# Own places for the expert results of a routed layer, and a gap behind every indirect transfer of five bodies

## The chip, the cores and the metric

The kernel runs on one core of one Trainium2 chip. The metric is the device time of one execution in microseconds (us), as the median of several runs. The kernel before takes 930.24 us (three runs, 926.34 to 932.70).

## The reference

Two layers on `x` of 4 x 1024 tokens of 128 numbers. Layer 0 is a differential attention times a gate from an FP4-rounded feed-forward; layer 1 is a linear attention times a gate from a mixture of experts. The change lies in the mixture of experts:

```
probs = softmax(x @ wg.T); topk_w, topk_idx = top_k(probs, 2)      # 8 experts, 2 for each token
topk_w = topk_w / sum(topk_w)
h1, h3 = x @ w1[e].T, x @ w3[e].T                                  # 128 -> 256, for each expert e
y[e] = (silu(h1) * h3) @ w2[e].T                                   # 256 -> 128
out = sum over the 2 chosen experts of weight * y[e]
x = x + attention * silu(out)
```

## The kernel before

The program is a row of phases with a barrier between them: setup, project, attention, linear, expert. The linear phase computes the layer-1 attention and the routing. The expert phase does the expert matrices and the final sum.

**Routing by scatter.** The four batches form two sets of two. For each set the tokens, each twice (once for each of its two experts), are sorted by expert into 39 tiles of 128 slots (`SLOTS`), padded for each expert. So there are 78 tiles. A row of 129 numbers (128 of the token and one that names where its result belongs) is written by `scatter_rows` (L932) to its slot in the DRAM tensor `slots`; one indirect transfer on the queue of GpSimd (POOL) writes 128 rows. Each set needs 32 of them. Those of set 0 and the first six of set 1 are issued in the linear phase; the other 26 (the list `later`) are issued in the expert phase.

**Bodies.** A body is six tiles (`BODY`), in two halves of three (`TRIO`); there are 13 bodies, numbered 0 to 12. For each tile s of body b: TensorE transposes the tile (`turn_x`, L1813), multiplies by both up matrices (`up`, L1822), ScalarE takes the tanh (L1769), VectorE makes the hidden tile in two steps (L1678, L1681), TensorE transposes it (`turn_a`, L1833) and multiplies by the down matrix (`down`, L1844), and VectorE copies the result out of PSUM (`keep_y`, L1694). Within a body the steps of neighbouring tiles are interleaved by hand: at step s, TensorE does `up(s)`, `turn_x(s+2)`, `turn_a(s-1)`, `down(s-2)`, in this order.

**Loads.** SyncE (SP) loads the halves of the next body with `load_next(b)`, which calls `load_tiles` (L925): half i of body b+1, once `turn_x` has read the old half and VectorE has copied its destinations (`keep_goal`, L1686). Tiles 36 to 38, the first half of body 6, are the last of set 0; the second half of body 6 is the first that holds rows of set 1. So its load, in `load_next(5, wait_rows=True)`, waits at L1580 for all 26 scatters of the list `later`.

**Sends.** `send(b, i)` on POOL sends the three result tiles of half i of body b to the DRAM tensor `expert_outputs`, with one indirect transfer each (L1636). The results lie in two buffers of three tiles, `y_out[i]`. Before a half is overwritten (in `keep_y`), and before its destinations are copied to `goal_now[i]` (L1631), there is a wait for the transfers of the same half one body earlier (`y_sent[i]`). Slots that hold no token are sent to one of 768 spare rows. The order of the queue of POOL is written out by hand: in bodies 0 to 4 (`EARLY`) some two or three scatters stand ahead of each half's sends, 26 in all, the last three of them ahead of `send(4, 1)`. Bodies 5 to 7 and 8 to 11 are hardware loops, body 12 is written out.

**Hands.** The results of set 0 are read back in four hands of four token tiles while bodies 8 to 11 run (`READY` = 8): SP loads them (`load_y`, L1585), POOL weighs one choice (`weigh_first`, L1642) and adds `x` (`add_x`, L1646), VectorE does the rest (L1698 to L1712), SP stores (`store`, L1589). Four more hands (`last_hands`) come after the last send, and end the kernel. `finish` (L1712) waits for the store of the hand before it.

**Memory.** `xn_all`, `v_all` and `w13_in` are three tiles of 4096 columns, which nothing reads any more in the expert phase.

## Time and profile before

| | us |
|---|---|
| median of 3 runs | 930.24 |
| the profiled execution | 931.66 |
| its span, first to last instruction | 928.8 |
| granted TensorE clock, mean | 0.873 of full |

The expert phase covers the span from 706 us on. The page of the profile gives the busy time of each engine, how each slice of the span looks, and the chain of work that ended last. The timeline lists instructions by start time; the number in brackets is the idle time of that engine just before, with what released it. "remote" there is a releaser that the trace doesn't know.

### The profile page before, as it was taken

Reading aid. Unit: us, or ns where it says so; the run is one execution under the profiler, and the core shown is the slowest. Engines: PE = TensorE matmul, PEld = TensorE weight load, DVE = VectorE, ACT = ScalarE, POOL = GpSimd, SP = SyncE. Lnnn points to the kernel's source line nnn. Section 1 sums busy time; section 2 is a strip of 40 time slices with the busy share of each in tenths; the row PEclk is TensorE's granted clock in tenths of the full one; section 3 lists DMA queues with packets and bytes.
Section 4 is the critical chain, followed back from the end, with each engine's and each line's share of the span. In section 5 each row is a group of like instructions: output and inputs, shape, how many; then the busy total and the mean of one; then the engine's idle time right before and its main releaser. Section 6 shows DMA issues by size and latency. Waiting matters only on the chain. (4 is left out here: it accounts for less than half of the span.)

```text
span 928.8 us, 14563 instructions
## 1 busy us (share of the span) xinstructions
PE 709.9 (76%) x4458; PEld 358.3 (39%) x4459; DVE 613.6 (66%) x1470; ACT 504.4 (54%) x911; POOL 443.6 (48%) x524
## 2 busy tenths in 40 slices
PE   3455539999999999999999956787367777898840
PEld 1234422333333333333333345675244444565520
DVE  3999972786868687868686655787163443467735
ACT  2367656777777777777787823233033332344431
POOL 0244433455656564646565521117713667456653
PEclk9777755999999999999999977778577999899975
DMA  5100029800000000000000010001201222233342
GB/s 131 42 24 23 12 69 191 123 24 23 24 23 23 23 23 23 23 23 16 6 23 24 1 47 24 23 24 41 74 24 40 72 71 63 61 92 114 99 113 59
DMA packets 58770, 45.32 MB, mean 49 GB/s; under 512 B 5960, under 2 KB 53392, under 8 KB 58736
## 3 DMA queue, kind: packets, MB, share of 16 engines
q1 hardware_dynamic: 51392, 34.97, 15.1%
q0 software_dynamic: 4544, 9.35, 3.0%
q10 hardware_dynamic: 2800, 0.58, 0.3%
q8 instruction: 17, 0.28, 0.1%
q14 instruction: 17, 0.14, 0.0%
HBM read 15.72 MB, written 16.59 MB: 35 GB/s over the span
## 5 line engine op out<-in xcount | busy, mean ns | idle before, releaser
L748 ACT ACTIVATE attend_prob<-attend_ps_s 128x1024 f32<-128x1024 f32 (+3 forms) x384 | 293.5, 816 | 95.6 <-PE attend_ps_s L848 93.1
L696 POOL TENSOR_TENSOR attend_prob<-attend_prob,attend_causal 128x256 f32<-128x256 f32 x256 | 202.3, 810 | 178.6 <-ACT attend_prob L748 177.3
L866 PE MATMUL attend_ps_o<-attend_prob,attend_v_slot 128*32 128x512 f32 (+3 forms) x1536 | 167.3, 509 | 0.0
L848 PE MATMUL attend_ps_s<-attend_qk_slot 32*128 32x512 f16 (+3 forms) x768 | 124.6, 339 | 21.9 <-ACT attend_prob L748 16.4
L1636 POOL DMA_INDIRECT expert_outputs<-expert_y_out,expert_goal_now x78 | 75.5, 968 | 64.8 <-issue 27.5
L848 PEld LDWEIGHTS attend_ps_s<-attend_qk_slot 32*128 32x128 f16 x768 | 34.8, 91 | 179.1 <-issue 86.4
L1822 PE MATMUL expert_ps_h<-w,expert_x_t 128*128 x156 | 91.3, 669 | 0.6 <-ACT expert_x_t L1756 0.6
L932 POOL DMA_INDIRECT slots<-rows,slot_index x64 | 61.6, 963 | 56.9 <-issue 56.9
L1769 ACT ACTIVATE expert_tanh<-expert_ps_h 128x256 f32<-128x256 f32 x78 | 30.0, 384 | 97.0 <-PE expert_ps_h L1822 67.1
L1844 PE MATMUL expert_ps_y<-w,expert_hidden_t 128*128 x312 | 54.3, 299 | 19.8 <-DVE expert_y_out L1694 14.1
L1678 DVE SCALAR_TENSOR_TENSOR expert_silu<-expert_tanh,expert_ps_h 128x256 f32<-128x256 f32 x78 | 32.7, 419 | 49.8 <-ACT expert_tanh L1769 30.7
L809 DVE SCALAR_TENSOR_TENSOR attend_hidden<-attend_gate_tanh,attend_ps_gate 128x352 f32<-128x352 f32 x32 | 16.7, 521 | 57.7 <-ACT attend_gate_tanh L752 57.7
L1844 PEld LDWEIGHTS expert_ps_y<-w,expert_hidden_t 128*128 128x128 f32 x312 | 43.0, 199 | 27.9 <-issue 26.1
L411 POOL TENSOR_TENSOR project_parts_k<-project_rotated_k,project_parts_k 128x1024 f16<-128x1024 f32 x8 | 17.1, 2132 | 57.2 <-ACT project_parts_k L453 57.2
L866 PEld LDWEIGHTS attend_ps_o<-attend_prob,attend_v_slot 128*32 128x32 f32 x1536 | 30.6, 108 | 34.6 <-issue 26.9
L1694 DVE COPY expert_y_out<-expert_ps_y 128x128 f32<-128x128 f32 x78 | 22.3, 286 | 25.6 <-remote 16.9
L1307 ACT ACTIVATE linear_qk_square<-linear_ps_c 128x512 f32<-128x512 f32 x16 | 9.5, 592 | 52.7 <-PE linear_ps_c L1411 27.8
L1760 ACT ACTIVATE expert_hidden_t<-expert_ps_a 128x256 f32<-128x256 f32 x78 | 30.2, 388 | 13.8 <-remote 7.4
L1833 PE MATMUL expert_ps_a<-ident,expert_hidden 128*128 128x128 f32 x156 | 31.5, 284 | 7.4 <-DVE expert_hidden L1681 5.0
L496 PE MATMUL project_ps_qkv<-att_w,project_xn_t 128*128 128x384 f32 x64 | 33.6, 689 | 4.4 <-issue 3.7
L1240 POOL TENSOR_TENSOR x<-x,linear_gated 128x1024 f32<-128x1024 f32 x4 | 9.4, 2359 | 53.6 <-DVE linear_gated L1072 53.5
L1681 DVE TENSOR_TENSOR expert_hidden<-expert_silu,expert_ps_h 128x256 f32<-128x256 f32 x78 | 32.8, 420 | 2.7
(252 smaller groups left out, 1367.6 us busy)
## 6 DMA issues: line engine op xcount, KB each, us to landing
attend_qk_slot<-qk_parts SPq DMA_DIRECT2D x16, 512.0 KB
slots<-attend_zeros SPq DMA_DIRECT2D x26, 193.5 KB
x_pairs<-slots SPq DMA_DIRECT2D x26, 193.5 KB
expert_y_in<-expert_outputs SPq DMA_DIRECT2D x8, 512.0 KB, 6.8
xn_all<-project_xn SPq DMA_DIRECT2D x8, 256.0 KB, 2.3
w_in<-L_ffn_w SPq DMA_DIRECT2D x4, 512.0 KB
rows<-rows SPq DMA_DIRECT2D x4, 512.0 KB
out<-expert_result SPq DMA_DIRECT2D x8, 256.0 KB, 2.3
```

Source lines behind the costliest of these rows:

```text
L496: ins = nc.tensor.matmul(qkv4[:, j, 0:3 * C], xn_t[odd][:, j * P:(j + 1) * P], m.att_w[:, 0:3 * C], start=True, stop=True)
L696: nc.gpsimd.tensor_tensor(part, part, bcast(causal, 1, 2), ALU.mult).then_inc(masked[n], 1)
L748: nc.scalar.activation(prob2[k % PROBS][:, :, 0:cols], s2[k % 2][:, :, 0:cols], ACT.Exp, scale=HD ** -0.5).then_inc(exp_made[k], 1)
L848: ins = nc.tensor.matmul(ps_s[k % 2][:, s * QC:(s + 1) * QC - off], qk_slot[slot][rows, T + j * P:T + (j + 1) * P], qk_slot[slot][rows, qc ...
L866: ins = nc.tensor.matmul(ps_o[RB * s:RB * (s + 1), off:QC], v4[slot][:, j, s], prob2[(2 * n + s // 2) % PROBS][:, s % 2, 0:QC - off], star ...
L932: pool.indirect_dma_start(m.slots, bass.IndirectOffsetOnAxis(m.slot_index[g][c][:, j:j + 1], 0), m.rows[c][:, t * ROW:(t + 1) * ROW], None ...
L1636: pool.indirect_dma_start(m.outputs, bass.IndirectOffsetOnAxis(goal_now[i][:, j:j + 1], 0), y_out[i][:, j * P:(j + 1) * P], None).then_inc ...
L1678: nc.vector.scalar_tensor_tensor(out=silu[c], in0=th[c], scalar=1.0, in1=ps_h[c][:, 0:EI], op0=ALU.add, op1=ALU.mult).then_inc(silu_made[s ...
L1681: nc.vector.tensor_tensor(act_e[c], silu[c], ps_h[c][:, EI:2 * EI], ALU.mult).then_inc(a_made[s], 1)
L1822: nc.tensor.matmul(ps_h[s % 3], x_t[s % 3], m.w13[:, ds(expert * (2 * EI), 2 * EI)], start=True, stop=True).then_inc(h_made[s], 1)
L1833: ins = nc.tensor.transpose(ps_a[s % 2][:, c * P:(c + 1) * P], act_e[s % 3][:, c * P:(c + 1) * P], m.ident)
L1844: ins = nc.tensor.matmul(ps_y[:, 0:P], act_t[s % 2][:, c * P:(c + 1) * P], m.w2[:, ds(expert * EI + c * P, P)], start=c == 0, stop=c == 1)
```

## The change

`y_out` becomes one tile `m.y_out` of 78 places of 128 columns, laid over the dead `xn_all`, `v_all` and `w13_in` (now parts of one tile). `keep_y` writes tile 6b+s to its own place, at an address from the loop's counter. The copies to `goal_now` and the waits for `y_sent` in `send` and `keep_y` go; the transfer reads its destinations from `goal`. Every slot has a spare row of its own (9984 rows in place of 768). The order of POOL is written out for all 13 bodies. In bodies 0 to 4 every send and every scatter is followed by `leave_gap`: a clear of the scratch tile `idle` (128 x 256, f32) and a wait for it. `READY` goes from 8 to 9, so the four hands run in bodies 9 to 12, and the last body does a hand too. SP waits for one semaphore for each set in place of one for each half.

```diff
-SPARE = BODY * P
+SPARE = SETS * SLOTS * P
-        READY = -(-SLOTS // SB) + 1
+        READY = -(-SLOTS // SB) + 2
-        y_out = [sb(f"y_out{i}", TRIO * P) for i in range(2)]
-        goal, spare = sb("goal", SETS * SLOTS, U32), sb("spare_row", BODY, U32)
-        goal_now = [sb(f"goal_now{i}", TRIO, U32) for i in range(2)]
+        idle = sb("idle", 2 * P)
+        goal, spare = sb("goal", SETS * SLOTS, U32), sb("spare_row", SETS * SLOTS, U32)
...
-            with eng.Fori(READY, READY + HANDS) as b:
+            with eng.Fori(READY, BODIES - 1) as b:
                 pairs(b, tok=b - READY)
-            for b in range(READY + HANDS, BODIES):
-                pairs(b, last=b == BODIES - 1)
+            pairs(BODIES - 1, last=True, tok=HANDS - 1)
...
-            for i in range(2):
-                sp.wait_ge(y_sent[i], 16 * TRIO * FIRST_SENT[i])
+            sp.wait_ge(y_sent[0], 16 * SLOTS)
...
-            for b in range(READY + HANDS - 1, BODIES - 1):
-                load_next(b)
-                store(0, b - READY - 1)
             for n in range(BODIES - 2 - READY, HANDS):
                 store(0, n)
-            for i in range(2):
-                sp.wait_ge(y_sent[i], 16 * TRIO * BODIES)
+            sp.wait_ge(y_sent[1], 16 * SLOTS)
...
+            def leave_gap():
+                nc.gpsimd.memset(idle, 0.0).then_inc(idled, 1)
+                pool.wait_ge(idled, next(gaps))
+
             def send(b, i):
                 pool.wait_ge(goal_kept[i], b + 1)
-                once(pool, y_sent[i], 16 * TRIO * b)
-                pool.sem_inc(send_go, 1)
-                nc.gpsimd.tensor_copy(goal_now[i], goal[:, ds(BODY * b + TRIO * i, TRIO)]).then_inc(goal_set[i], 1)
-                pool.wait_ge(goal_set[i], b + 1)
                 for j in range(TRIO):
+                    t = BODY * b + TRIO * i + j
                     pool.wait_ge(y_kept[TRIO * i + j], b + 1)
                     pool.sem_inc(send_go, 1)
-                    pool.indirect_dma_start(m.outputs, bass.IndirectOffsetOnAxis(goal_now[i][:, j:j + 1], 0),
-                                            y_out[i][:, j * P:(j + 1) * P], None).then_inc(y_sent[i], 16)
+                    pool.indirect_dma_start(m.outputs, bass.IndirectOffsetOnAxis(goal[:, t:t + 1], 0),
+                                            m.y_out[:, t * P:(t + 1) * P], None).then_inc(y_sent[t // SLOTS], 16)
+                    if b < EARLY:
+                        leave_gap()
...
             for b in range(EARLY):
                 for i in range(2):
                     n = 2 * b + i
-                    scatter_rows(pool, m, later[n * len(later) // (2 * EARLY):(n + 1) * len(later) // (2 * EARLY)], rows_scattered)
+                    for row in later[n * len(later) // (2 * EARLY):(n + 1) * len(later) // (2 * EARLY)]:
+                        scatter_rows(pool, m, [row], rows_scattered)
+                        leave_gap()
                     send(b, i)
-            with pool.Fori(EARLY, READY) as b:
+            for b in range(EARLY, BODIES):
+                hand = 0 <= b - READY < HANDS
+                if hand:
+                    weigh_first(0, b - READY)
                 for i in range(2):
                     send(b, i)
...
+                if hand:
+                    add_x(0, b - READY)
...
             def keep_y(b, s):
                 dve.wait_ge(y_made[s], b + 1)
-                if s % TRIO == 0:
-                    once(dve, y_sent[s // TRIO], 16 * TRIO * b)
-                nc.vector.tensor_copy(y_out[s // TRIO][:, s % TRIO * P:(s % TRIO + 1) * P], ps_y[:, 0:P]).then_inc(y_kept[s], 1)
+                nc.vector.tensor_copy(m.y_out[:, ds((BODY * b + s) * P, P)], ps_y[:, 0:P]).then_inc(y_kept[s], 1)
...
-        m.x, m.xn, m.v = (sb(n, BATCH * T) for n in ("x", "xn_all", "v_all"))
+        m.x, shared = sb("x", BATCH * T), sb("xn_v_w13", 3 * BATCH * T)
+        m.xn, m.v, m.w13_in = (shared[:, i * BATCH * T:(i + 1) * BATCH * T] for i in range(3))
+        m.y_out = shared[:, 0:SETS * SLOTS * P]
```

## Rows read from the trace of the kernel before

**Rows 1.** The page: busy time of each engine (share) xinstructions
```profile
PE 709.9 (76%) x4458; PEld 358.3 (39%) x4459; DVE 613.6 (66%) x1470; ACT 504.4 (54%) x911; POOL 443.6 (48%) x524
```

**Rows 2.** Stretches of the expert phase: from:to, length, busy time by engine, clock, DMA
```profile
714.79:799.08 84.29, 63.20 (x268) 38.19 (x268) 34.05 (x100) 26.44 (x90) 53.88 (x65) 0.92 0.23 66
799.08:834.80 35.72, 35.29 (x174) 22.08 (x173) 22.20 (x65) 16.22 (x57) 19.57 (x25) 1.00 0.28 81
834.80:888.51 53.71, 47.40 (x217) 28.70 (x217) 39.71 (x96) 23.30 (x76) 34.51 (x39) 0.97 0.35 99
```

**Rows 3.** Timeline of POOL, 722 to 726 us: start, us, engine, line, operation, [idle before]
```profile
722.32 0.96 POOL L932 DMA_INDIRECT slots<-rows,slot_index  x1 [0.30 <-issue]
723.29 0.20 POOL L1631 COPY expert_goal_now<-expert_goal 128x3 uint32<-128x3 uint32 x1
724.33 0.97 POOL L1636 DMA_INDIRECT expert_outputs<-expert_y_out,expert_goal_now  x1 [0.84 <-POOL expert_goal_now L1631]
```

**Rows 4.** Waits from 714.79 to 799.08 us: total us, times, longest
```profile
DVE expert_y_out L1694 <- remote: 16.9, 8, 3.7
...
PE expert_ps_y L1844 <- DVE expert_y_out L1694: 14.1, 7, 3.8
```

**Rows 5.** Timelines of TensorE and of VectorE, 728 to 733 us
```profile
728.49 1.12 PE L1822 MATMUL expert_ps_h<-w,expert_x_t 128*128 x2
...
729.53 0.42 DVE L1681 TENSOR_TENSOR expert_hidden<-expert_silu,expert_ps_h 128x256 f32<-128x256 f32 x1
732.31 0.29 DVE L1694 COPY expert_y_out<-expert_ps_y 128x128 f32<-128x128 f32 x1 [2.36 <-remote]
```

**Rows 6.** Timeline of ScalarE and of POOL in the linear phase, 641 to 674 us
```profile
673.41 0.60 ACT L1307 ACTIVATE linear_qk_square<-linear_ps_c 128x512 f32<-128x512 f32 x1 [22.58 <-remote]
...
641.70 0.99 POOL L932 DMA_INDIRECT slots<-rows,slot_index  x1 [0.17 <-issue]
...
670.77 0.96 POOL L932 DMA_INDIRECT slots<-rows,slot_index  x1 [0.30 <-issue]
```

**Rows 7.** POOL by line and shape, whole span: count, busy us, mean ns, idle before
```profile
L717 POOL MEMSET attend_v_slot<- 128x1024 f32 x2 | 1.9, 967 | 0.0
...
L1646 POOL TENSOR_TENSOR expert_result<-expert_result,x 128x512 f32<-128x512 f32 x8 | 11.4, 1424 | 3.4 <-DVE expert_result L1712 3.3
...
L1254 POOL MEMSET linear_tokens_before<- 128x128 f32 x1 | 0.2, 200 | 0.0
L1255 POOL MEMSET linear_experts_before<- 128x64 f32 x1 | 0.1, 147 | 0.0
```

**Rows 8.** Timeline of POOL: the first send and the last scatter
```profile
714.79 0.98 POOL L1636 DMA_INDIRECT expert_outputs<-expert_y_out,expert_goal_now  x1 [4.34 <-DVE expert_y_out L1694]
...
788.96 0.95 POOL L932 DMA_INDIRECT slots<-rows,slot_index  x1 [0.30 <-issue]
```

**Rows 9.** SP's wait at L1580; then SP's and TensorE's timelines at body 6
```profile
SPq L1580 <- DVE expert_goal L1686: 8.2, 1, 8.2
...
799.70 0.38 SPq L925 DMA_DIRECT2D x_pairs<-slots  x1
...
806.53 0.14 PEld L1813 LDWEIGHTS expert_ps_x<-ident,x_pairs 128*128 128x128 f32 x1 [0.24 <-issue]
```

**Rows 10.** The last send and SP's next load; a store of 256 KB from the page (KB, us to landing)
```profile
895.77 0.97 POOL L1636 DMA_INDIRECT expert_outputs<-expert_y_out,expert_goal_now  x1 [0.42 <-issue]
...
898.06 2.19 SPq L1585 DMA_DIRECT2D expert_y_in<-expert_outputs  x3
...
out<-expert_result SPq DMA_DIRECT2D x8, 256.0 KB, 2.3
```

**Rows 11.** The stretch after a pause of TensorE: length, busy times by engine, granted clock
```profile
792.60:799.40 6.80, 5.96 (x16) 3.69 (x17) 2.62 (x8) 1.76 (x6) 2.43 (x4) 0.50 0.06 22
```

**Rows 12.** VectorE by line and shape, 690 to 929 us: count, busy us, mean ns, idle
```profile
L1686 DVE TENSOR_TENSOR expert_goal<-x_pairs,expert_spare_row 128x3 uint32 x22 | 9.0, 411 | 0.6 <-issue 0.6
...
L1686 DVE TENSOR_TENSOR expert_goal<-x_pairs,expert_spare_row 128x3 uint32<-128x3 uint32 x4 | 1.5, 372 | 0.0
```

More of the change, by code:

```diff
@@ L3 @@
+import itertools
 import math
@@ L1534, in expert_phase @@
                 "x_turned", "xt_kept", "h_made", "th_made", "silu_made", "a_made", "a_turned", "at_kept", "y_made", "y_kept"))
-        goal_kept, goal_set, y_sent = ([sem(f"{n}{i}") for i in range(2)] for n in ("goal_kept", "goal_set", "y_sent"))
+        goal_kept = [sem(f"goal_kept{i}") for i in range(2)]
+        y_sent = [sem(f"y_sent{g}") for g in range(SETS)]
         y_loaded, weighed1, weighed2, summed, ty_made, gated, scaled, res_made, stored = (
@@ L1538, in expert_phase @@
                 "y_loaded", "weighed1_", "weighed2_", "summed", "ty_made", "gated", "scaled", "res_made", "stored"))
-        send_go = sem("send_go")
+        send_go, idled = sem("send_go"), sem("idled")
         y_v = m.outputs[SPARE:SPARE + 2 * BATCH * T].rearrange("(n p) c -> p n c", p=P)
@@ L1653, in _ @@
                     n = 2 * b + i
-                    scatter_rows(pool, m, later[n * len(later) // (2 * EARLY):(n + 1) * len(later) // (2 * EARLY)], rows_scattered)
+                    for row in later[n * len(later) // (2 * EARLY):(n + 1) * len(later) // (2 * EARLY)]:
+                        scatter_rows(pool, m, [row], rows_scattered)
+                        leave_gap()
                     send(b, i)
-            with pool.Fori(EARLY, READY) as b:
+            for b in range(EARLY, BODIES):
+                hand = 0 <= b - READY < HANDS
+                if hand:
+                    weigh_first(0, b - READY)
                 for i in range(2):
                     send(b, i)
-            with pool.Fori(READY, READY + HANDS) as b:
-                weigh_first(0, b - READY)
-                for i in range(2):
-                    send(b, i)
-                add_x(0, b - READY)
-            for b in range(READY + HANDS, BODIES):
-                for i in range(2):
-                    send(b, i)
+                if hand:
+                    add_x(0, b - READY)
             for k, n in last_hands:
@@ L1907, in build @@
         m.eps_ln, m.eps_rms, m.eps_head = sb("eps_ln", 1), sb("eps_rms", 1), sb("eps_head", 1)
-        m.w13_in, m.wg_in = sb("w13_in", EXPERTS * 2 * EI), sb("router_in", P)
+        m.wg_in = sb("router_in", P)
         with ExitStack() as layer0:
```

6 lines of the change are left out of this document (3 added, 3 removed).

## The prediction

> **What bounds the kernel now.** I read the page first. TensorE is busy for 76% of the span and POOL for 48% [rows 1], so over the whole kernel TensorE looks like the bound. The change touches only the expert phase, so I cut that phase into stretches at the first send of a body [rows 2]. Bodies 5 to 7 take 35.72 us, 11.9 us each, with TensorE busy for 35.29 us of it: there TensorE is the bound. Bodies 0 to 4 take 84.29 us, 16.9 us each, although they compute the same. So 84.29 - 5 x 11.9 = 24.8 us are lost there, and this is the change's ground. Bodies 8 to 11 take 53.71 us, 13.4 us each, since they carry the hands.
>
> Two things are peculiar to bodies 0 to 4. First, POOL issues 26 scatters beside 30 sends. Its timeline [rows 3] shows the beat: a transfer takes 0.96 us, and the next follows 0.30 us later, 1.26 us from start to start. Where a copy of destinations stands between (723.29) and the next transfer must wait for it, the copy starts at once, takes 0.20 us, and the transfer starts 0.84 us after its end: 2.01 us from start to start. 56 transfers of 1.26 us and ten copies of some 0.75 us make 78 us: POOL is nearly full in these 84 us. Second, VectorE and ScalarE stand still without a reason in the program. The waits show 16.9 us in which the copy of a result waited for something the trace doesn't know, and TensorE waited 14.1 us for that copy [rows 4]. I looked at one: VectorE stands from 729.95 to 732.31 [rows 5]. It isn't the wait for `y_sent`: the copy there is of the second tile of a half, which doesn't have that wait, and the down matmuls that it reads stand in TensorE's order ahead of the up matmul that started at 728.49 [rows 5]. In the linear phase the same is seen at its largest: POOL issues 24 scatters at a beat of 1.26 us from 641.70 to 670.77, and ScalarE stands for 22.58 us until 673.41 [rows 6]. In bodies 5 to 7, where POOL waits for results between its sends, there is no such wait. So strings of transfers back to back hold up the other engines, and a gap between them is a plausible cure.
>
> **What the change removes.** The waits for `y_sent` cost nothing now, by the reading above; without them TensorE may run ahead of POOL. Ten copies in bodies 0 to 4 go, at 2.01 - 1.26 = 0.75 us each on POOL. If the gaps also cure the pauses, TensorE does a body in 11.9 us and stands in front of the second half of body 6 at 806.53 [rows 9] minus 24.8 = 781.7 us.
>
> **What it adds: 56 gaps on POOL.** The clear of 128 x 256: 64 columns take 147 ns, 128 take 200, 1024 take 967 [rows 7]; between the last two that is 0.856 ns a column, so 256 take 200 + 128 x 0.856 = 310 ns. The send after it has to wait for it, as the send after the copy does now, and I take the same 0.84 us [rows 3]. So from one transfer to a following send: 0.96 + 0.31 + 0.84 = 2.11 us. To a following scatter there is no such row. Its bounds are the 0.84 us of the copy and the 0.30 us of a transfer that waits for nothing [rows 3]: 2.11 or 1.57 us. I take 2.11, since the row with a wait on POOL's own work is the nearest; the other end is a rival.
>
> The Trainium skill (Advanced Engine Details and Errata, Sequencer and Instruction Queues) says that an engine's instruction is pushed into a queue and waits for its semaphores there, while later ones are read. By that the scatter would be prepared during the wait, and the lower price would hold; for a send, which has a semaphore increment of the sequencer between wait and transfer, it would not. The sum by that rule is the first rival's.
>
> **Who waits for it.** The second half of body 6 holds the first rows of set 1, and its load waits for all 26 scatters (L1580). Now that is free: the last scatter starts at 788.96 [rows 8], and at L1580 SP still waits 8.2 us for VectorE [rows 9]. With the gaps it is not. From the first send (714.79, set by TensorE's first result and not moved) to the last scatter stand 50 steps: the followers are 26 sends and 24 scatters. At 2.11 us each: 714.79 + 105.5 = 820.3. Until SP sees it landed, 2.3 us (last send 895.77, SP's load 898.06 [rows 10]); the load itself, 193.5 KB, 2.3 us, by a store of 256 KB [rows 10]. TensorE has the tiles at 824.9 in place of 806.53: **+18.4 us**. Behind the waiting SP stand only the loads of body 7 and on, which are in time. TensorE, in program order, stands in front of this transpose, and with it the down matmul of the last tile of body 5 and all that follows. Whether the gaps cure the pauses is without weight: with 24.8 us of pauses or without, TensorE comes too early.
>
> **After the wait.** Three smaller terms. (1) Clock: after a pause TensorE is granted 0.50, 1.2 GHz, for 6.8 us, in which 5.96 us are busy [rows 11]; that work takes half the time at 2.4 GHz: **+3.0**. (2) POOL still owes `send(4, 1)` with gaps (6.3 us) and the results of body 5: it ends the gaps at about 829 and then sends back to back until it has caught up with TensorE. A backlog of 6 tiles against 1.98 us (11.9 / 6) for each new one is gone after 6 x 1.26 / (1 - 1.26 / 1.98) = 21 us at most. A string of that kind costs 24.8 us in 84 now; in 21 us 6 us. From below nothing, since the backlog may be smaller. I take **+3**. (3) The last body gets a hand, and SP must store hands 2 and 3 before it loads the last hands: `add_x` of hand 3 (1.4 us [rows 7]) comes after the last send, and a store of 256 KB goes ahead of the loads. The landing of the last send hides some of it. I take **+1.5**, with 0 and 3.7 (1.4 and a whole store of 2.3 [rows 10]) as ends.
>
> At nothing: the hands move from bodies 8 to 11 to bodies 9 to 12 and cost there what they cost now (53.71 - 4 x 11.9 = 6 us [rows 2]); their first load waits for 39 sends, which are out near 850, when SP comes to it. The computed address in `keep_y` is covered by VectorE's slack, 22.2 busy of 35.7 us [rows 2]; uncovered it is bounded by what an address from a counter costs `keep_goal`, 411 against 372 ns [rows 12], 78 times: 3 us. The copies and waits that fall in bodies 5 to 12 lie on POOL beside a busy TensorE. A clear might hold VectorE through the SBUF port that both use (the Trainium skill, SBUF — State Buffer, Who interferes with whom, calls it an exclusive lock); no row here has the two together, and at that time VectorE has slack.
>
> **The sum.** 931.66 (the profiled execution) + 18.4 + 3.0 + 3 + 1.5 = 957.6. The profiled execution is 1.4 above the median, so the median becomes 956.
>
> **Rivals.**
> (a) The wait of a scatter costs 0.30 in place of 0.84. 24 x 0.54 = 13.0 us less: 943. For it: a scatter has no increment between wait and transfer. Against it: no row.
> (b) The other side: the clear and its wait vanish in the 0.30 us between two transfers, so that the beat stays 1.27 us (0.96 + 0.31). Then the last scatter starts at 714.79 + 63.5 = 778.3 and its tiles are there at 782.9, when TensorE wants them if the pauses are cured: 23.6 us earlier than 806.53. 931.7 - 23.6 + 1.5 - 1.4 = 908. It decides below a mean beat of 1.47 us, where the tiles come at 792.9, the gain is 13.6 and, less 3.0 for the clock and 1.5, is 1% of the time. Against it stands every copy with a wait in the bodies before, at 0.84 us.
> (c) The preparation of a transfer is hidden for sends and scatters alike, beat 1.57: tiles at 714.79 + 78.5 + 4.6 = 797.9, gain 8.6, less 3.0 and 1.5: 926. With 3 for a string of sends: 929. No change that can be measured.
> (d) The strings after the gaps are worse than 3 us, as in the linear phase (22.58 of 29 us [rows 6]). Until the backlog is gone, 6 tiles x 1.26 = 8 us of standstill in place of 3, and the address (3) and the tail (2 more) at their upper ends: 956 + 5 + 3 + 2 = 966.
>
> **How the numbers follow.** My forecast has 0.52, (a) 0.23, (b) 0.05, (c) 0.11, (d) 0.09. The range goes from between (c) and (a), 936, to 966: it leaves out (b), (c) and little of (d). About 1% is what a measurement tells from no change. Slower by over 1%, above 939.5: forecast, (a) and (d), 0.84. Within 1%: (c), 0.11. Faster: (b), 0.05.
>
> **What would show it.** After: 56 clears of about 0.31 us, the beat 2.11 us in bodies 0 to 4, the last scatter at about 820, SP waiting at L1580 for transfers and not for VectorE, TensorE idle for 20 to 40 us in front of the second half of body 6, a clock of 0.50 behind that, no waits on an unknown releaser in bodies 0 to 4. It is wrong if the last scatter starts before about 800 (the price of a gap), or if TensorE gains in the bodies behind it, which no row promises.

## The result, and the profile after

| | before | after |
|---|---|---|
| median | 928.29 us (924.56 to 932.70, 4 runs) | 942.98 us (942.20 to 943.84, 4 runs) |
| ratio, 95% interval | | 1.0169 [1.0135, 1.0203] |
| profiled execution | 931.66 us | 943.36 us |
| its span | 928.8 us | 941.7 us |
| mean granted TensorE clock | 0.873 | 0.869 |

The change makes the kernel slower by 1.7%. The median of 942.98 is inside the range of 936 to 966, 13 us below the forecast of 956, and on the value of rival (a), 943. The first line below is the page of the kernel after, busy time by engine, and answers to [rows 1]: POOL has 30 instructions more and TensorE the same number. The second is from the table by line and shape of POOL between 703 and 813 us: the 56 clears.

```profile
PE 697.9 (74%) x4458; PEld 351.5 (37%) x4459; DVE 613.3 (65%) x1470; ACT 504.0 (54%) x911; POOL 456.8 (49%) x554
...
L1625 POOL MEMSET expert_idle<- 128x256 f32 x56 | 18.3, 326 | 0.0
```

POOL's timeline of the kernel after, which answers to [rows 3], has the beat of a gap:

```profile
726.91 0.97 POOL L1635 DMA_INDIRECT expert_outputs<-xn_v_w,expert_goal  x1 [0.86 <-POOL expert_idle L1625]
727.88 0.33 POOL L1625 MEMSET expert_idle<- 128x256 f32 x1
728.49 0.97 POOL L933 DMA_INDIRECT slots<-rows,slot_index  x1 [0.28 <-POOL expert_idle L1625]
729.45 0.33 POOL L1625 MEMSET expert_idle<- 128x256 f32 x1
730.06 0.97 POOL L933 DMA_INDIRECT slots<-rows,slot_index  x1 [0.28 <-POOL expert_idle L1625]
...
805.28 0.97 POOL L933 DMA_INDIRECT slots<-rows,slot_index  x1 [0.28 <-POOL expert_idle L1625]
```

A clear takes 0.33 us. A send (L1635) starts 0.86 us after its end, a scatter (L933) 0.28 us after it. So from the start of a transfer to that of a following send it is 2.16 us, and to that of a following scatter 1.57 us. The first send starts at 711.41, the last scatter at 805.28, 93.9 us later (before 74.2, [rows 8]).

Who waits for that last scatter: the waits of SP between 700 and 850 us, the waits of TensorE and ScalarE between 711 and 812 us (total us, times, longest), then the weight load that ends TensorE's wait. They answer to [rows 9].

```profile
SPq L1579 <- DMA slots<-rows,slot_index: 46.2, 1, 46.2
...
PEld expert_ps_x L1811 <- DMA x_pairs<-slots: 37.1, 1, 37.1
ACT expert_x_t L1754 <- issue: 36.3, 1, 36.3
...
810.32 0.18 PEld L1811 LDWEIGHTS expert_ps_x<-ident,x_pairs 128*128 128x128 f32 x1 [37.09 <-DMA x_pairs<-slots]
```

SP no longer waits for VectorE at this place (8.2 us before), but 46.2 us for the scatters. TensorE stands for 37.09 us in front of the second half of body 6. These are three stretches of the kernel after (from:to, length, busy time of PE, PEld, DVE, ACT, POOL, clock, DMA share, GB/s), to be held against [rows 2]:

```profile
711.41:773.20 61.79, 60.96 (x299) 38.31 (x299) 36.63 (x113) 28.21 (x100) 42.68 (x66) 1.00 0.24 67
773.20:810.32 37.12, 0.86 (x2) 0.03 (x2) 1.11 (x3) 0.38 (x1) 25.28 (x39) 0.55 0.14 45
810.32:830.00 19.68, 14.46 (x54) 9.06 (x55) 6.00 (x18) 5.23 (x17) 11.50 (x14) 0.76 0.20 63
```

From the first send until it has to stop, TensorE is busy for 60.96 of 61.79 us at the full clock. With 54 matmuls to a body, the 299 in this stretch are five and a half bodies, 11.2 us each; before it was 16.9 us each, busy for 63.20 of 84.29. The waits of VectorE in this stretch have no line with an unknown releaser, where [rows 4] had 16.9 us. The pauses of bodies 0 to 4 are gone, as the change's gaps suggest. Nothing comes of it, since TensorE reaches the gate 33 us earlier than before and then waits 37.

After the gate POOL catches up. Its timeline, VectorE's from 820 us on, and the waits of the stretch 810 to 830 us:

```profile
813.92 0.97 POOL L1635 DMA_INDIRECT expert_outputs<-xn_v_w,expert_goal  x1 [0.86 <-POOL expert_idle L1625]
815.19 0.96 POOL L1635 DMA_INDIRECT expert_outputs<-xn_v_w,expert_goal  x1 [0.30 <-issue]
...
824.05 0.96 POOL L1635 DMA_INDIRECT expert_outputs<-xn_v_w,expert_goal  x1 [0.30 <-issue]
...
822.53 0.29 DVE L1692 COPY xn_v_w<-expert_ps_y 128x128 f32 x1 [3.76 <-remote]
...
826.90 0.29 DVE L1692 COPY xn_v_w<-expert_ps_y 128x128 f32 x1 [2.46 <-remote]
```

Nine sends start 1.27 us apart, without a gap, and in the second half of that string and just behind it VectorE stands again for 3.76 and 2.46 us, released by something that the profile doesn't name.

**What VectorE waits for in a pause.** The trace also holds the time at which each recorded update of a semaphore took effect, and there the releaser can be found. This is TensorE's timeline of the kernel before, around the pause that the prediction looked at:

```profile
727.87 0.71 PE L1844 MATMUL expert_ps_y<-w,expert_hidden_t 128*128 x4 [0.87 <-DVE expert_y_out L1694]
...
729.45 0.27 PE L1813 MATMUL expert_ps_x<-ident,x_pairs 128*128 128x128 f32 x1
730.00 0.44 PE L1833 MATMUL expert_ps_a<-ident,expert_hidden 128*128 128x128 f32 x2 [0.28 <-issue]
```

The last of the four down matmuls ends at 728.57 by the profile (its ends of matmuls are modelled). The update of the semaphore that it increments comes at 732.29, 3.71 us later, and VectorE's copy starts at 732.31 [rows 5]. In between TensorE starts further matmuls, up to 730.17. So in a pause VectorE and ScalarE wait for TensorE's semaphores, which are late. The same holds in the whole stretch from 706 to 870 us of the kernel before: 46 of the 227 recorded updates by matmuls come more than 0.6 us after the matmul's end, 5.6 us at most, while each of the 368 by VectorE, ScalarE and GpSimd comes within 0.02 us. In the kernel after it is 9 of 205, none before 818 us. Whether the matmul's result is late as well, or its semaphore alone, the trace doesn't tell.

**The books.** In the span, 941.7 - 928.8 = 12.9 us. First send: 711.41 against 714.79, -3.4; it lies before the change's ground. From the first send to the gate: 810.32 - 711.41 = 98.9 against 806.53 - 714.79 = 91.7, +7.2. From the gate to the last send: 908.38 - 810.32 = 98.1 against 895.77 - 806.53 = 89.2, +8.8. From there to the end: 33.3 against 33.0, +0.3. The sum is 12.9.

### The profile page after: what moved, and what is told of

Read it like the earlier page. It is cut to its first block and busy times, and to the rows that moved or that the text cites. A ratio compares the mean times of both kernels' runs of the same rounds, so it can differ in the third digit from the quotient of the medians.

```text
span 941.7 us, 14554 instructions
## 1 busy us (share of the span) xinstructions
PE 697.9 (74%) x4458; PEld 351.5 (37%) x4459; DVE 613.3 (65%) x1470; ACT 504.0 (54%) x911; POOL 456.8 (49%) x554
## 5 line engine op out<-in xcount | busy, mean ns | idle before, releaser
L1635 POOL DMA_INDIRECT expert_outputs<-xn_v_w,expert_goal x78 | 76.2, 977 | 72.5 <-DVE xn_v_w L1692 25.2
L933 POOL DMA_INDIRECT slots<-rows,slot_index x64 | 61.9, 967 | 58.2 <-issue 51.3
L1820 PE MATMUL expert_ps_h<-w,expert_x_t 128*128 x156 | 88.9, 653 | 0.6 <-ACT expert_x_t L1754 0.6
L1811 PE MATMUL expert_ps_x<-ident,x_pairs 128*128 128x128 f32 x78 | 22.9, 297 | 45.0 <-DMA x_pairs<-slots 36.3
L810 DVE SCALAR_TENSOR_TENSOR attend_hidden<-attend_gate_tanh,attend_ps_gate 128x352 f32<-128x352 f32 x32 | 16.7, 522 | 57.2 <-ACT attend_gate_tanh L753 57.2
L1692 DVE COPY xn_v_w<-expert_ps_y 128x128 f32 (+1 forms) x78 | 22.3, 285 | 47.4 <-PE expert_ps_y L1842 40.7
L1842 PEld LDWEIGHTS expert_ps_y<-w,expert_hidden_t 128*128 128x128 f32 x312 | 42.4, 197 | 13.1 <-issue 11.1
L1754 ACT ACTIVATE expert_x_t<-expert_ps_x 128x128 f32<-128x128 f32 x78 | 21.2, 272 | 44.8 <-issue 36.3
L497 PE MATMUL project_ps_qkv<-att_w,project_xn_t 128*128 128x384 f32 x64 | 35.8, 725 | 4.4 <-issue 3.7
L1811 PEld LDWEIGHTS expert_ps_x<-ident,x_pairs 128*128 128x128 f32 x78 | 11.5, 149 | 72.3 <-DMA x_pairs<-slots 37.1
```

What stands on the lines that cost most here:

```text
L497: ins = nc.tensor.matmul(qkv4[:, j, 0:3 * C], xn_t[odd][:, j * P:(j + 1) * P], m.att_w[:, 0:3 * C], start=True, stop=True)
L933: pool.indirect_dma_start(m.slots, bass.IndirectOffsetOnAxis(m.slot_index[g][c][:, j:j + 1], 0), m.rows[c][:, t * ROW:(t + 1) * ROW], None ...
L1635: pool.indirect_dma_start(m.outputs, bass.IndirectOffsetOnAxis(goal[:, t:t + 1], 0), m.y_out[:, t * P:(t + 1) * P], None).then_inc(y_sent[ ...
L1811: nc.tensor.transpose(ps_x[s % 2][:, 0:P], x_tile(s), m.ident).then_inc(x_turned[s], 1)
L1820: nc.tensor.matmul(ps_h[s % 3], x_t[s % 3], m.w13[:, ds(expert * (2 * EI), 2 * EI)], start=True, stop=True).then_inc(h_made[s], 1)
L1842: ins = nc.tensor.matmul(ps_y[:, 0:P], act_t[s % 2][:, c * P:(c + 1) * P], m.w2[:, ds(expert * EI + c * P, P)], start=c == 0, stop=c == 1)
```

## The experiments

All are edits of the kernel after unless said otherwise. They ran on three chips, each beside the kernel before. The kernel before took 893.8 us on the first chip (`e1` to `e4`), 928.4 on the second (`before_again`, `after_again`, `e5`, `e6`) and 926.9 on the third (`e7` to `e10`). That spread matters, as the first run shows. Each chip was used at one time only, so a property of the chip and its state at that time can't be told apart; "chip" below means either. "The gate" is TensorE's start on the second half of body 6.

### e1_no_gaps: the change without its gaps

```diff
-                    if b < EARLY:
-                        leave_gap()
...
-                        leave_gap()
```

> The changed kernel without any of its 56 gaps. The beat of POOL goes back to 1.26 us, so the last scatter starts at about 711.4 + 50 x 1.26 = 774.5 and its tiles are there at 779.5, in place of 810.3. Theory (the gaps cured the pauses of VectorE and ScalarE, own places did not): the pauses return, TensorE comes to the second half of body 6 near 800 as in the kernel before, and the time is that of the kernel before or some us less: 922 to 932. Rival (the waits for y_sent caused the pauses, so own places alone cure them): TensorE waits until 779.5 at most, 31 us less than the changed kernel: 912.

Measured: 882.69 us against 893.82, ratio 0.9887 [0.985, 0.9923]. The last scatter starts 64.1 us after the first send. The stretch between the two, and the waits of SP and TensorE around it:

```profile
688.20:752.30 64.10, 62.10 (x301) 38.54 (x299) 37.68 (x115) 28.74 (x101) 47.90 (x51) 1.00 0.28 82
...
SPq L1579 <- DMA slots<-rows,slot_index: 16.4, 1, 16.4
...
PE expert_ps_x L1808 <- DMA x_pairs<-slots: 6.4, 1, 6.4
```

POOL's transfers stand 1.26 us apart here, back to back, and TensorE is busy for 62.10 of 64.10 us. There is no pause, in the expert phase or in the linear phase, where the kernel before had 22.58 us [rows 6]. Of the 304 recorded updates by matmuls between 679 and 840 us none comes later than 0.02 us. So on this chip the strings do not hold the other engines, and the kernel before is faster here by some 34 us than on the other two. Two things follow. Own places, without the gaps, are worth 1.1% on such a chip (there is no trace of the kernel before on it, so where the 11 us come from is open). And even a beat of 1.26 us is a little too slow for the gate, by 6.4 us, when TensorE isn't disturbed.

### e2, e3, e4: the price of the gap, on the chip without pauses

`e2_gaps_at_scatters` keeps the 26 gaps behind scatters and drops the 30 behind sends.

```diff
-                    if b < EARLY:
-                        leave_gap()
```

> The changed kernel with a gap after each scatter only (26 gaps), none after a send. Followers of a gap are at 1.57 (scatter) or 2.16 (send): after each group of scatters one send at 2.16, so 50 steps are about 15 scatters at 1.57, 9 sends at 2.16, 9 scatters after a send at 1.26 and 17 sends at 1.26: 76 us, last scatter at 787.5, tiles at 792.5, 18 us earlier than now. Theory (the pauses need a string of several transfers back to back, and three or four in a row are too few): no pauses, time 943 - 18 = 925. Rival (every transfer without a gap adds its pause): pauses of some us come back, but hidden before the wait at body 6 unless they exceed 19 us; then also 925. So the time says what the gate costs, and the waits on an unknown releaser in bodies 0 to 4 say which theory holds: under 3 us in all, or over 8.

Measured: 899.31 us, ratio 1.0056 [1.0031, 1.0081]; last scatter 75.9 us after the first send, TensorE at the gate after a wait of 18 us.

`e3_attached_wait` keeps all gaps, moves the wait for the clear to just ahead of the next transfer, and drops the increment of the sends in bodies 0 to 4.

```diff
-                pool.wait_ge(idled, next(gaps))
+                made[0] += 1
...
-                    pool.sem_inc(send_go, 1)
+                    if b < EARLY:
+                        end_gap()
+                    else:
+                        pool.sem_inc(send_go, 1)
```

> The changed kernel with all 56 gaps, but in bodies 0 to 4 without the semaphore increment between the wait and the transfer of a send, so that the wait for the clear is carried by the transfer itself, as it is for the scatters. Theory (the 0.87 us before a send is the preparation of the transfer, which starts only after a wait that stands in an instruction of its own): the sends' step falls from 2.16 to 1.57, the last scatter starts at 711.4 + 50 x 1.57 = 790, tiles at 795, 15 us earlier: 928. Rival (the 0.87 is the wait for VectorE's result or a price of reading the destinations, whatever carries the wait): no change, 943. The pauses in bodies 0 to 4 should stay away, since the idle time between transfers is still 0.6 us.

Measured: 912.59 us, ratio 1.0213 [1.0159, 1.0268]; last scatter 92.3 us after the first send. POOL's timeline:

```profile
699.35 0.96 POOL L933 DMA_INDIRECT slots<-rows,slot_index  x1 [0.28 <-POOL expert_idle L1625]
700.31 0.33 POOL L1625 MEMSET expert_idle<- 128x256 f32 x1
701.47 0.96 POOL L1643 DMA_INDIRECT expert_outputs<-xn_v_w,expert_goal  x1 [0.84 <-POOL expert_idle L1625]
702.44 0.33 POOL L1625 MEMSET expert_idle<- 128x256 f32 x1
703.58 0.96 POOL L1643 DMA_INDIRECT expert_outputs<-xn_v_w,expert_goal  x1 [0.81 <-POOL expert_idle L1625]
```

The price of a send hardly moved, from 0.86 or 0.87 us to between 0.80 and 0.84. The trace's single instructions say why. A transfer carries at most one wait in itself; the others stand in a semaphore instruction of their own ahead of it. In the kernel after the scatters carry the wait for the clear, while a send carries none: all its waits stand in the instruction that makes the increment. In this run a send carried the wait for its result (`y_kept`), which had long been met, and the wait for the clear stood in a separate instruction; the transfer starts 0.76 us after the end of that one. So the increment is worth at most 0.07 us, and the run did not test what it was made for. `e7` below does.

`e4_narrow_clear` is the kernel after with a clear of one column.

```diff
-        idle = sb("idle", 2 * P)
+        idle = sb("idle", 1)
```

> The changed kernel with a scratch tile of one column, so that the clear takes about 0.1 us in place of 0.33; waits as they are. 50 x 0.22 = 11 us less to the last scatter: 932, if the gate at body 6 is what costs. Theory for the pauses (it is the break in the string that cures them, not its length in clear time): none in bodies 0 to 4. Rival (POOL must be kept from transfers for some 0.6 us each time): the scatters' gap is now 0.37 us against 0.30 without one, and pauses of several us come back in the stretches of scatters, hidden behind the gate in part.

Measured: 907.77 us, ratio 1.014 [1.0096, 1.0185]; a clear takes 0.11 us, the 0.28 and 0.87 us behind it stay, and the last scatter starts 82.9 us after the first send.

On this chip, with no pauses to cure, the gate sets most of the time. What `e2` and `e4` were to tell of the pauses (whether gaps behind the scatters are enough, or a narrow gap) could not be seen here.

| | last scatter, us after first send | TensorE waits at the gate, us | median, us |
|---|---|---|---|
| e1, no gaps | 64.1 | 6.4 | 882.69 |
| e2, gaps behind scatters | 75.9 | 18.2 | 899.31 |
| e4, narrow clear | 82.9 | 25.0 | 907.77 |
| e3, all gaps | 92.3 | 34.5 | 912.59 |

From `e1` to `e3` the last scatter comes 28.2 us later and the time rises by 29.9. Part of it lies ahead of the gaps: in the profiled executions the expert phase starts at 678.9 us in `e1`, 681.8 in `e2`, 682.0 in `e3` and 685.7 in `e4`, which no edit here explains. Without that the time rises by 13.7 (`e2`), 18.2 (`e4`) and 26.7 us (`e3`), for a last scatter that is 11.8, 18.8 and 28.2 us later.

### before_again and after_again: both kernels on a second chip

> The kernel before, unchanged, for its trace. The four runs without a pause of an unknown releaser stood beside a kernel before of 893.8 us, 34 less than 928.3. Theory (the pauses are a property of the chip or of its state, and not of the kernel alone): where the kernel before takes about 894, its trace shows no such pause, its linear phase is some 25 us shorter (the expert phase starts near 682 and not at 706), and bodies 0 to 4 are bound by POOL's queue at about 78 us and not 84. Rival (it was the kernel's own transfers that differed in the changed kernels): pauses of 15 us and more stand in its linear phase here too.

> The changed kernel, unchanged. Where there are no pauses the gaps have nothing to cure, so all that is left is their price at the gate of body 6: last scatter 93.9 us after the first send, as against some 68 in the kernel before without pauses, 20 us later for the first tiles of set 1. Ratio to the kernel before 1.023 to 1.030 (about 916 beside 893.8). Where pauses are there: 1.017 as before.

Measured: 928.63 us, ratio 1.000 [0.9974, 1.0027], and 944.76 us, ratio 1.0169 [1.0125, 1.0214]. The waits of VectorE in the kernel before (600 to 790 us) have the pauses of both phases:

```profile
DVE linear_logits L1104 <- remote: 23.8, 1, 23.8
DVE expert_y_out L1694 <- remote: 19.8, 11, 3.0
```

In the kernel after, between its first send and the gate, VectorE has no wait with an unknown releaser, and the last scatter starts 93.7 us after the first send. So the pauses are there on this chip in the kernel before, the gaps take them away in bodies 0 to 4, and the loss is the 1.7% of the result again.

### e5 and e6: no gaps, the scatters brought forward

`e5_scatters_early` drops the gaps and issues the 26 scatters in the halves of bodies 0 to 2, so that the gate is open early.

```diff
-                    for row in later[n * len(later) // (2 * EARLY):(n + 1) * len(later) // (2 * EARLY)]:
+                    for row in later[n * len(later) // 6:(n + 1) * len(later) // 6] if n < 6 else []:
```

> The changed kernel without gaps, and with the 26 scatters spread over the halves of bodies 0 to 2 in place of 0 to 4; the sends fall behind by as much, which their own places allow. The last scatter has 15 sends ahead of it in place of 27, so it starts some 15 us earlier, about 50 us after the first send, before TensorE asks for the tiles (62.5 us after the first send). Theory (the gate is all that held TensorE in the kernel without gaps): its 6.4 us of waiting go, 876 beside 893.8. Rival (another limit, the sends that lag behind, hands or POOL's queue, takes its place): the same as without gaps, 882.

Measured: 929.76 us, ratio 1.0007 [0.9984, 1.003]. The last scatter starts 53.4 us after the first send, and SP never waits for it. But TensorE came to the gate only 93.1 us after the first send. The stretch while POOL sends back to back, the stretch from there to the gate, and the waits of the first:

```profile
715.20:771.80 56.60, 35.35 (x137) 20.97 (x136) 17.08 (x50) 12.92 (x46) 35.40 (x37) 0.77 0.21 61
771.80:808.70 36.90, 36.45 (x168) 23.14 (x169) 20.99 (x64) 16.28 (x57) 18.19 (x19) 0.94 0.24 68
...
ACT expert_tanh L1764 <- remote: 16.7, 3, 8.1
DVE xn_v_w L1689 <- remote: 13.4, 4, 6.6
PE expert_ps_y L1839 <- DVE xn_v_w L1689: 11.8, 3, 6.8
```

During the strings TensorE is busy for 35.35 of 56.60 us, with pauses of up to 8.1 us; behind them for 36.45 of 36.90. Moving the transfers together moves the pauses with them; nothing is won.

`e6_early_ready8` is `e5` with the hands in bodies 8 to 11 again, as in the kernel before.

```diff
-        READY = -(-SLOTS // SB) + 2
+        READY = -(-SLOTS // SB) + 1
```

> The last kernel, and the hands back in bodies 8 to 11. The last body loses its hand: the stretch from the gate to the last send was 90 to 91 us with the hands in bodies 9 to 12 and 88.8 with them in 8 to 11, and the tail 33.2 against 33.0. Theory (the later hands cost these 2 us): 874 beside 893.8. Rival (set 0's results are not out in time for body 8, since POOL's sends lag): TensorE or VectorE waits in body 8, 876 or more.

Measured: 929.21 us, ratio 1.0023 [0.9995, 1.0051]. Which bodies have the hands makes no difference here that can be measured.

### e7_clear_wait_carried: all 56 gaps, the clear's wait in the transfer

As `e3`, but in the code the wait for the clear is written first, ahead of the waits for the destinations and the result. The first wait written proved to be the one that the transfer carries (the text below calls that place "behind the other waits"); the wait for the result goes into an instruction of its own.

```diff
+                    if b < EARLY:
+                        end_gap()
+                    if j == 0:
+                        pool.wait_ge(goal_kept[i], b + 1)
                     pool.wait_ge(y_kept[TRIO * i + j], b + 1)
```

> The changed kernel with all its 56 gaps, but the wait for a gap's clear is the one that the transfer itself carries, for sends too: the wait for the clear stands behind the other waits of a send in the order that puts it into the transfer, and the sends of bodies 0 to 4 lose their semaphore increment. Theory (what a gap costs depends on who carries the wait): a send after a clear then costs what a scatter after a clear costs in the changed kernel, 0.96 + 0.33 + 0.28 = 1.57 us in place of 2.16. 50 steps of 1.57: last scatter 78.5 us after the first send in place of 93.9, the tiles of the second half of body 6 some 5 us behind that, TensorE idle for some 21 us in place of 37. About 15 us less than the changed kernel: 928, a ratio of 1.00 where the kernel before takes 928. Rival (the preparation of a send is dear whoever carries the wait, since it carries another pattern than a scatter): no change against the changed kernel, last scatter 94 us after the first send, 943, ratio 1.017.

Measured: 928.04 us, ratio 0.9996 [0.9971, 1.0021]. POOL's timeline, the wait at the gate, and the stretch from the first send to the gate's wait:

```profile
730.36 0.96 POOL L1644 DMA_INDIRECT expert_outputs<-xn_v_w,expert_goal  x1 [0.28 <-POOL expert_idle L1625]
731.32 0.33 POOL L1625 MEMSET expert_idle<- 128x256 f32 x1
731.92 0.97 POOL L1644 DMA_INDIRECT expert_outputs<-xn_v_w,expert_goal  x1 [0.28 <-POOL expert_idle L1625]
...
PE expert_ps_x L1821 <- DMA x_pairs<-slots: 20.9, 1, 20.9
...
710.90:773.20 62.30, 61.47 (x304) 38.83 (x303) 36.94 (x113) 28.82 (x102) 50.79 (x79) 1.00 0.26 74
```

A send now starts 0.28 us after the clear, as a scatter does. The last scatter starts 79.0 us after the first send, the ratio is 0.9996 where the kernel after had 1.0169 (some 15 us), and the 1.57 us from start to start still cure the pauses: TensorE is busy for 61.47 of 62.30 us. So the 0.86 us of a send are not the send's own; they come with the wait for the clear standing in a separate instruction. That they are the transfer's preparation, which begins only when that instruction has passed, fits all these rows but is not itself seen in them. The strings of sends behind the gaps keep their pauses: from the gate on 8 updates by matmuls are late, by up to 5.1 us.

### e8, e9, e10: early scatters with gaps

`e8_early_narrow_gaps` has both: carried waits, a clear of one column, gaps up to body 7, the 26 scatters in the first five halves, and the hands in bodies 8 to 11.

```diff
-        idle = sb("idle", 2 * P)
+        idle = sb("idle", 1)
...
-                    if b < EARLY:
+                    if b < 8:
                         leave_gap()
...
-                    for row in later[n * len(later) // (2 * EARLY):(n + 1) * len(later) // (2 * EARLY)]:
+                    for row in later[max(0, 5 * n + 1) if n else 0:5 * n + 6]:
+                        end_gap()
```

> Own places, a clear of one column after each transfer of bodies 0 to 7 whose wait the next transfer carries, and the 26 scatters brought forward into the first five halves; hands in bodies 8 to 11 as in the kernel before. Theory (the gap need not be long, only the transfers must not stand back to back, and the loss of the change is the delay of the last scatter): the beat is 0.96 + 0.11 + 0.28 = 1.35 us, the last scatter comes some 43 us after the first send, before TensorE wants its tiles at 62 to 73, and there are no pauses in bodies 0 to 7: 11.2 us a body, second half of body 6 started 73 us after the first send in place of 92. Some 20 us and the 9 us of pauses after the gate less than the changed kernel and more: about 895 to 905 where the kernel before takes 928, ratio 0.965 to 0.975. Rival (the gap has to be long; 0.39 us between transfers are as good as the 0.30 of no gap): pauses of VectorE and ScalarE of up to 8 us come back in bodies 0 to 4 and the second half of body 6 starts 92 us after the first send, 925 to 930, ratio 1.00. On a chip whose kernel before takes 894 there is nothing to cure: about 880, ratio 0.985.

`e10_early_wide_gaps` is `e8` with the clear at its full width.

```diff
-        idle = sb("idle", 1)
+        idle = sb("idle", 2 * P)
```

> The kernel with early scatters, its clears 256 columns wide as in the changed kernel in place of one column; waits carried by the transfers. Beat 0.96 + 0.33 + 0.28 = 1.57 us; last scatter some 58 us after the first send, its tiles at 63, still ahead of TensorE without pauses at 73. Theory (the place of the scatters and not the gap's length decides): as with one column, within 5 us, and no pauses in bodies 0 to 7. If only a long gap cures: some 20 us less than with one column, 895 to 905 beside 925. Rival (VectorE is held by the wide clears themselves): operations of VectorE in bodies 0 to 7 longer than in the kernel before by more than 10%, and TensorE over 11.6 us a body.

Measured: `e8` 927.33 us, ratio 0.9999 [0.997, 1.0028]; `e10` 916.65 us, ratio 0.9888 [0.9853, 0.9922]. First `e8`: POOL's timeline, the stretch from the first send to the end of the pauses, and VectorE's waits.

```profile
729.23 0.96 POOL L1648 DMA_INDIRECT expert_outputs<-xn_v_w,expert_goal  x1 [0.28 <-issue]
730.20 0.11 POOL L1629 MEMSET expert_idle<- 128x1 f32 x1
730.59 0.96 POOL L1648 DMA_INDIRECT expert_outputs<-xn_v_w,expert_goal  x1 [0.28 <-issue]
...
715.50:766.00 50.50, 29.83 (x115) 16.76 (x115) 14.65 (x43) 11.20 (x38) 35.40 (x66) 0.79 0.22 65
...
DVE xn_v_w L1706 <- remote: 21.3, 7, 5.9
```

Then `e10`: its stretches from the first send to the gate, from there until VectorE stops, and beyond; then two waits, of SP and of VectorE.

```profile
713.00:774.50 61.50, 60.63 (x297) 37.92 (x295) 36.19 (x110) 28.04 (x99) 50.66 (x79) 1.00 0.27 78
774.50:798.60 24.10, 23.82 (x120) 15.12 (x119) 14.19 (x43) 11.10 (x39) 19.93 (x31) 1.00 0.24 72
798.60:812.10 13.50, 2.22 (x12) 1.13 (x10) 1.53 (x4) 1.38 (x5) 11.00 (x19) 0.66 0.31 97
...
SPq L1585 <- DMA expert_outputs<-xn_v_w,expert_goal: 16.3, 1, 16.3
...
DVE expert_y_in L1710 <- DMA expert_y_in<-expert_outputs: 12.0, 1, 12.0
```

The two kernels differ in the width of a clear alone. With 0.11 us of it, transfers start 1.35 us apart and the pauses stay: 29.83 us busy of 50.50. With 0.33 us they start 1.57 us apart, and the pauses are gone: 60.63 of 61.50. In `e8` 30 updates by matmuls are late up to 870 us, by up to 7.8 us; in `e10` none is. TensorE passes the gate of `e10` 61.1 us after the first send, without a wait; before it took 91.7. Of these 30 us, `e10` keeps a third. POOL, at 1.57 us and more scatters ahead, is far behind TensorE; the first hand of body 8 needs the 39 sends of set 0, SP waits 16.3 us for them, VectorE 12.0 us for SP's load, and TensorE behind VectorE. The change's `READY` of 9 would ask for the hand 11.2 us later. That wasn't run; if all of the 12.0 us but 0.8 went, it would be some 905 us, an estimate. A second wait of VectorE, 6.4 us for POOL's weighing of a hand, follows on the first and is not in it.

`e9_linear_gaps_too` is `e8` with a narrow clear and a carried wait ahead of every scatter of the linear phase too.

```diff
+            def gapped(row, done):
+                nc.gpsimd.memset(lidle, 0.0).then_inc(lidled, 1)
+                pool.wait_ge(lidled, next(count))
+                scatter_rows(pool, m, [row], done)
```

> The kernel with early scatters and narrow gaps, and a clear of one column with a wait also ahead of each of the scatters of the linear phase, which in the kernel before stand back to back beside a standstill of 18 to 22 us of VectorE, ScalarE and TensorE. Theory (the standstill has the same cause as the pauses of the expert phase, and a narrow gap cures it): the expert phase starts some 20 us earlier, near 682 in place of 702 to 706; about 875 where the kernel before takes 928, ratio 0.945. If the linear phase is held by something else: as the kernel without these gaps. On a chip whose kernel before takes 894: within 3 us of the kernel without them.

Measured: 923.37 us, ratio 0.996 [0.9931, 0.9989], 4 us below `e8`. The expert phase starts at 697.5 us in place of 706.7 in the two profiled executions. (`e7` and `e10`, with the linear phase of `e8`, start it at 702.4 and 702.9, so the gain is nearer to 5 us, like the 4 us of the medians.) The longest waits of ScalarE for an unknown releaser, between 636 and 690 us, in `e8` and then in `e9`:

```profile
ACT linear_qk_square L1308 <- remote: 24.0, 1, 24.0
```

```profile
ACT attn_out L1338 <- remote: 6.9, 1, 6.9
```

The standstill of the linear phase is of the same kind: in the kernel before, the update that ends ScalarE's 22.58 us [rows 6] comes 16.8 us after the end of TensorE's matmul. A narrow gap breaks it into shorter pieces but doesn't end it; here too narrow gaps don't cure. The 20 us expected didn't come. Wide gaps in the linear phase weren't run.

## Why the prediction was right, and where it was off

**What bounds the kernel.** Right, on a chip with pauses: they go with the strings of transfers, and gaps cure them, to 11.2 us a body where the prediction took 11.9. The 11.9 divided the stretch between first sends by three, but its 174 matmuls [rows 2] are 3.2 bodies, 11.1 us each. And VectorE and ScalarE were not held up themselves, as the prediction has it; they waited for TensorE's semaphores, which came late. That the matmuls stood ahead in TensorE's order did not show that their semaphores had come. What no row of the trace could show is that this is a matter of the chip. `e1` ran on one where back-to-back transfers cost the other engines nothing; there the gaps are pure loss (`e3` against `e1`, 30 us, of which 3 lie ahead of the expert phase).

**A gap to a send.** Predicted 0.96 + 0.31 + 0.84 = 2.11, measured 0.97 + 0.33 + 0.86 = 2.16 us. The interpolated clear was 0.02 short.

**A gap to a scatter.** This step failed. The prediction took 2.11 us and kept 1.57 as the lower end; it is 1.57. 24 of them are 13.0 us less, 26 sends at 2.16 are 1.3 more: 105.5 - 13.0 + 1.3 = 93.8, measured 93.9. The argument "the row with a wait on POOL's own work is the nearest" compared what the wait is for. What counts is where it stands: in a scatter the transfer itself carries it, in a send a semaphore instruction ahead of the transfer does. `e7` shows this: against `e3`, which has no increment either, it changes the order of a send's waits alone, and the price falls from between 0.80 and 0.84 us to 0.28 (the two ran on different chips; scatters pay 0.28 us on both). Rival (a) had the right size; it named the increment as the reason, but `e3`, without the increment, pays 0.80 to 0.84 still. By the rule cited in the prediction (the Trainium skill, Advanced Engine Details and Errata, Sequencer and Instruction Queues), an engine's instruction is pushed into a queue and waits for its semaphores there; the trace agrees, with 0.28 us from the clear's end to a scatter. What a wait in an instruction of its own costs, 0.86 us here, that rule does not give.

**The gate.** The mechanism was right: SP waits for scatters and no longer for VectorE, TensorE stands for 37 us (20 to 40 had been named), and the cure of the pauses is worth nothing, since TensorE only comes earlier to a closed gate. The cure itself was larger than predicted: TensorE comes to the gate at 773.2, not at 781.7. The size of the delay was +18.4 and is +7.2: 11.6 us from the last scatter's time (105.5 against 93.9), less 0.4 for its landing and load (5.0 us against 4.6).

**After the gate.** Clock +3.0 and strings +3, together 6; measured 8.8. It can be divided by the stretches, an estimate from their mean clocks: from 810.32 to 817.10 TensorE is busy throughout at a mean clock of 0.70 (it starts at 0.50, 1.2 GHz, after its idle 37 us, and is at 1.00, 2.4 GHz, from 815 on), a loss of 0.30 x 6.78 = 2.0 us; from 817.10 to 830.00 it is busy for 7.68 of 12.90, a loss of 5.2 us for the pauses, at a mean clock of 0.79, which is 1.6 us more. The clock term, 3.0, was 1.0 too large for the wait at the gate and lacked the 1.6 that the string's pauses bring with them. The string itself is shorter than its bound (11 us, not 21) and dearer than predicted: 5.2 us in place of 3, towards rival (d).

**The tail.** +1.5 predicted, +0.3 measured: near the low end of its range. That the last send hides the hand's work is the likely reason, not one that a run tested.

**Rival (b)**, the gap that vanishes, would have needed the clear to lie in the 0.30 us between two transfers. It doesn't: every clear lies beyond the transfer, and 0.28 us come after it even where the wait is carried. Rival (c), both cheap, is what `e7` built: 928.04, where it had said 926 to 929.

So the sum of the steps was 25.9 us; measured it is 12.9 with 3.4 of luck ahead of the first send (in `after_again` against `before_again` the first send comes 1.6 us later instead). Of the gap between the two, 11.2 us are the gate's delay, mainly by one price taken 24 times; the terms behind it missed by +2.8 and -1.2.

## What to carry to other kernels

A cure is worth what the next gate lets through: before slowing a queue to free an engine, look for what that queue releases, and bring that forward first (`e10`, 1.1% faster than before; `e7`, with gaps of the same length in bodies 0 to 4 and late scatters, is no faster). When a wait must stand between two transfers of one queue, arrange for the transfer to carry it; in an instruction of its own it cost 0.58 us more each time, 15 us in all. And compare kernels on more than one chip where a pause has no releaser that the profile names: own places without gaps were 1.1% faster on one chip, and own places without gaps and with early scatters no different on another. Last, where the profile names no releaser, look for the semaphore's update itself: here it points at TensorE, which looked like the victim.

## What the runs showed of the hardware

**Late semaphores of TensorE beside strings of indirect transfers, on some chips.** Of the three chips of the experiments two have them and one has not; the same kernel takes 928.4 and 926.9 us on the ones, 893.8 on the other. Pauses of VectorE and ScalarE appear during a string or just behind it, up to 8.1 us each in the expert phase, and an idle time of 23.8 us in the linear phase. In all profiles with pauses it is updates by matmuls that are late (in the expert phase of `e5` 23 of 224, up to 11.0 us), and none by VectorE, ScalarE or GpSimd. Why a string delays them isn't known. The Trainium skill (SBUF — State Buffer, Who interferes with whom) says that a DMA never contends with a compute engine, and that ScalarE has ports of its own. The 16.7 and 13.4 us for which ScalarE and VectorE stand in `e5` beside such a string look like the contrary, but the trace doesn't show them to be one: both wait for TensorE's semaphores, and VectorE's copy takes 0.29 us in and out of a pause.

**The length of the gap decides.** 1.26 and 1.35 us from start to start leave the pauses, 1.57 cures them (`e5`, `e8`, `e10`). Whether it is the rest between two transfers or their mean rate that counts wasn't separated, nor whether a wide clear does something that a wait of the same length wouldn't. It does not hold up VectorE: beside the wide clears of `e10` VectorE's copies take 0.28 to 0.29 us. Why the chips differ stays open.
